# Graph attention with layer norm on one core: the last group of edges in two parts, and blocks of nodes finished four turns behind instead of five

## The reference

```python
Q, K, V = (x @ WQ, x @ WK, x @ WV)           # 8 heads of 16
E = edge_attr @ WE
score = exp(clip(sum_d(K[src] * Q[dst] * E) / 4, -5, 5))       # one per edge and head
h = segment_sum(V[src] * score, dst) / (segment_sum(score, dst) + 1e-6)
out = layernorm(x + h)
```

## Time and profile before

| | before |
|---|---|
| median of three executions | 2052.68 us |
| profiled execution, its own time | 2051.81 us |
| its span | 2050.0 us |
| POOL busy | 1531.1 us (75%), 1629 instructions |
| PE busy | 1521.4 us (74%) |
| DVE busy | 1488.4 us (73%) |
| ACT busy | 1386.6 us (68%) |
| DMA, mean rate | 174 GB/s |
| mean granted clock of PE | 0.892 of full |

### The profile page before, as it was taken

How to read it: one execution, slowest core, us unless ns; L and a number is a source line. 1 busy time by engine, 2 the same in 40 slices (tenths; PEclk the granted TensorE clock), 3 DMA queues, 4 the chain that set the end, 5 groups by cost and what they waited for, 6 DMA issues and landing times.

```text
span 2050.0 us, 40006 instructions
## 1 busy us (share of the span) xinstructions
PE 1521.4 (74%) x10440; PEld 1267.1 (62%) x10441; DVE 1488.4 (73%) x3809; ACT 1386.6 (68%) x3716; POOL 1531.1 (75%) x1629
## 2 busy tenths in 40 slices
PE   7788887778787776776677767677776777778674
PEld 6566666666666665665565556566665656666564
DVE  5577777878787776777677767767776776777676
ACT  4478786768777766666666666666666666666663
POOL 7777777777777777777777777777777777777774
PEclk9889898999899989889989989988889989888887
DMA  9668666666666665566566556656655655555552
GB/s 296 202 193 240 171 180 169 178 172 181 170 180 177 172 167 166 166 171 168 166 167 170 168 163 169 173 166 167 166 169 162 173 167 172 162 171 166 166 167 83
DMA packets 281410, 356.31 MB, mean 174 GB/s; under 512 B 144640, under 2 KB 177615, under 8 KB 281186
## 3 DMA queue, kind: packets, MB, share of 16 engines
q0 software_dynamic: 76864, 209.29, 35.3%
q1 hardware_dynamic: 203746, 144.18, 25.7%
q10 hardware_dynamic: 576, 0.26, 0.0%
HBM read 337.59 MB, written 15.97 MB: 172 GB/s over the span
## 4 chain that ended last, share of the span: by engine, by line
PE 24%; issue 21%; DVE 19%; POOL 17%; DMA 10%; DVEq 8%; ACT 0%; SPq 0%; POOLq 0%; ACTq 0%
POOL kv L560 17%; PE psW L712 13%; DMA kv<-kv_table,src_idx 9%; DVEq L286 6%; DVE msg L1105 6%; DVE acc L1121 5%; PE psE L691 4%; DVE prod L1089 3%; PE psT L675 3%; DVEq L1121 2%; PE psF L683 1%; PE psE L635 1%; DVE score L1094 1%; DVE newton L1159 1%; DMA q_table<-q_stage 1%
## 5 line engine op out<-in xcount | busy, mean ns | idle before, releaser
L560 POOL DMA_INDIRECT kv<-kv_table,src_idx x1580 | 1495.2, 946 | 485.6 <-issue 416.1
L712 PE MATMUL psW<-msg,hot 128*128 128x136 f32 x3224 | 539.0, 317 | 485.0 <-DVE msg L1105 483.9
L712 PEld LDWEIGHTS psW<-msg,hot 128*128 128x128 f32 x3224 | 462.3, 214 | 534.1 <-issue 509.2
L1084 DVE TENSOR_TENSOR prod<-kv,psE 128x512 f32<-128x512 f32 x403 | 275.5, 684 | 368.4 <-issue 186.3
L851 ACT ACTIVATE hot<-iota,local 128x128 f32<-128x128 f32 x1612 | 508.7, 386 | 0.0
L691 PE MATMUL psE<-w_e,attrT 128*128 128x128 f32 x3224 | 502.3, 302 | 0.0
L691 PEld LDWEIGHTS psE<-w_e,attrT 128*128 128x128 f32 x3224 | 423.6, 205 | 106.5 <-issue 106.5
L873 ACT ACTIVATE psW<-clipped 128x32 f32<-128x32 f32 x403 | 81.0, 201 | 571.4 <-DVE clipped L1100 564.3
L1121 DVE TENSOR_TENSOR acc<-psW,acc 64x136 f32 x806 | 238.0, 295 | 110.1 <-PE psW L712 102.2
L856 ACT ACTIVATE hot<-hot,one 128x512 f32<-128x512 f32 x403 | 291.0, 722 | 13.1
L1089 DVE TENSOR_TENSOR prod<-prod,psQ 128x512 f32<-128x512 f32 x403 | 277.1, 688 | 12.8 <-PE psQ L701 0.2
(11 more groups left out here) (118 smaller groups left out, 546.0 us busy)
## 6 DMA issues: line engine op xcount, KB each, us to landing
attr<-in_edge_attr_dram SPq DMA_DIRECT2D x403, 256.0 KB
kv<-kv_table,src_idx POOLq DMA_INDIRECT x1580
q_near<-q_table SPq DMA_DIRECT2D x403, 32.0 KB
kv_table<-kv SPq DMA_DIRECT2D x12, 512.0 KB, 4.9
q_table<-q_stage SPq DMA_DIRECT2D x12, 384.0 KB, 3.2
hot<-in_x_dram SPq DMA_DIRECT2D x12, 256.0 KB, 5.2
xT<-in_x_dram SPq DMA_DIRECT2D x8, 384.0 KB
out_dram<-xT SPq DMA_DIRECT2D x45, 64.0 KB
```

Source lines behind the costliest of these rows:

```text
L560: nc.gpsimd.indirect_dma_start(out=kv[:, g % RINGS, t, :], out_offset=None, in_=kv_table, in_offset=bass.IndirectOffsetOnAxis(ap=src_idx[: ...
L712: last = nc.tensor.matmul(psW[:, g % 2, 0:MW], hot[:, g % HOTS, t, :], msg[:, g % MSGS, t, :], start=(t == 0), stop=(t == TILES - 1))
L1084: nc.vector.tensor_tensor(tiles, kv[:, u, :, 0:dim], psE[:, g % 2, :].rearrange("p (t d) -> p t d", d=dim), ALU.mult).then_inc(ke, 1)
```

## The change

- The last group (402) is worked in two parts, tiles 0 to 2 and tile 3, on DVE, ACT and PE. `last_scores` and `last_messages` are `scores` and `messages` on the tiles of one part. The gather of tile 3 has a semaphore of its own, kv_last; its exponentials go to psT, as psW's bank is in use. The tail of DVE's program is ordered anew by two `meanwhile` functions.
- LAG becomes 4: 46 blocks are finished in the loop, block w in turn w + 4, and LATE becomes 3. The table's base is written 2(1 - LAG), the same number as before; the cap 2 EARLY becomes 92. DVE waits for `added` ahead of a block's first stage, and for the block's third stage ahead of the next group's addition.
- DVE loads the number of strays together with the last half windows, SP loads redo_cell ahead of its wait for the last blocks.

```diff
-LAG = 5
+LAG = 4
...
+        def last_exp_scores(part):
+            if part == 0:
+                return exp_scores(G - 1)[:, 0:TILES - 1, :]
+            return psT[:, 0:HEADS].rearrange("p (t h) -> p t h", h=HEADS)
...
@@ SP's program @@
+            redo = sp.value_load(redo_cell, min_val=0, max_val=G)
             sp.wait_ge(finished, (EARLY + 1) * STAGES)
...
-            with sp.If(sp.value_load(redo_cell, min_val=0, max_val=G) > 0):
+            with sp.If(redo > 0):
...
@@ POOL's program @@
-                           [[2, B_LAST], [0, TURN]], base=2 * (2 - LAG), channel_multiplier=0)
+                           [[2, B_LAST], [0, TURN]], base=2 * (1 - LAG), channel_multiplier=0)
...
+                    landed = kv_last if g == G - 1 and t == TILES - 1 else kv_in[g % RINGS]
...
@@ PE's program @@
+            def sum_last():
+                pe.wait_ge(hot_ok, G)
+                pe.wait_ge(added, G - 2)
+                for t in range(TILES):
+                    if t == 0:
+                        pe.wait_ge(heads_ok, G)
+                        pe.wait_ge(msg_ok, G)
+                    elif t == TILES - 1:
+                        pe.wait_ge(heads_ok, G + 1)
+                        pe.wait_ge(msg_ok, G + 1)
+                    last = nc.tensor.matmul(psW[:, (G - 1) % 2, 0:MW], hot[:, (G - 1) % HOTS, t, :],
+                                            msg[:, (G - 1) % MSGS, t, :], start=(t == 0), stop=(t == TILES - 1))
+                last.then_inc(sums, 1)
...
-            sum_messages(G - 1)
+            sum_last()
...
@@ ACT's program @@
+            def exponentials_last(part):
+                tiles = slice(0, TILES - 1) if part == 0 else slice(TILES - 1, TILES)
+                act.wait_ge(clip, G + part)
...
+                nc.scalar.activation(last_exp_scores(part), scores, ACT.Exp, scale=SCALE).then_inc(exp_ok, 1)
+                if part == 0:
+                    act.wait_ge(sums, G - MSGS)
+                nc.scalar.activation(msg[:, (G - 1) % MSGS, tiles, dim:MW], scores, ACT.Exp, scale=SCALE)\
+                    .then_inc(heads_ok, 1)
...
@@ DVE's program @@
+            def last_scores(part, meanwhile):
+                g = G - 1
+                u, tiles = g % RINGS, slice(0, TILES - 1) if part == 0 else slice(TILES - 1, TILES)
...
+                if part == 0:
+                    dve.wait_ge(e_mm, G)
+                    dve.wait_ge(kv_in[u], KV_WITHOUT_LAST)
+                else:
+                    dve.wait_ge(kv_last, 16)
...
             def step(g, windows, w=None):
                 def meanwhile(i):
+                    if w is not None and (u, i) == (1, 0):
+                        dve.wait_ge(finished, w * STAGES + 3)
                     if i == 0 and g >= 2:
                         add_sums(g - 2, windows)
                     if i == 1 and g >= 1:
                         messages(g - 1)
+                    if w is not None and 3 * u + i == 0:
+                        dve.wait_ge(added, g - 1)
                     if w is not None and 3 * u + i < STAGES:
                         finish(3 * u + i, w, 1, window_y[:, :, :], finished, w * STAGES)
...
             windows = load_windows(B_LAST * TURN - 2, G - B_LAST * TURN + 2)
-            for g in range(B_LAST * TURN, G):
+            strays = dve.value_load(table[0:1, STRAYS, G:G + 1], min_val=0, max_val=G)
+            for g in range(B_LAST * TURN, G - 1):
                 step(g, windows[g - B_LAST * TURN])
-            messages(G - 1)
-            add_sums(G - 2, windows[-2])
+            def meanwhile_first(i):
+                if i == 0:
+                    add_sums(G - 3, windows[-3])
+                elif i == 1:
+                    messages(G - 2)
+            def meanwhile_second(i):
+                if i == 0:
+                    last_messages(0)
+                elif i == 1:
+                    add_sums(G - 2, windows[-2])
+            last_scores(0, meanwhile_first)
+            last_scores(1, meanwhile_second)
+            last_messages(1)
             add_sums(G - 1, windows[-1])
...
-            dve.wait_ge(table_ok, 1)
-            with dve.If(dve.value_load(table[0:1, STRAYS, G:G + 1], min_val=0, max_val=G) > 0):
+            with dve.If(strays > 0):
```

More of the change, by code:

```diff
@@ L241, in graph_attention_layernorm @@
         kv_in = [sem(f"kv_in{i}") for i in range(RINGS)]
+        kv_last = sem("kv_last")
         go = sem("go")
@@ L292, in exp_scores @@
             return psW[:, g % 2, GROUP // 2:GROUP // 2 + TILES * HEADS].rearrange("p (t h) -> p t h", h=HEADS)
+        def last_exp_scores(part):
+            if part == 0:
+                return exp_scores(G - 1)[:, 0:TILES - 1, :]
+            return psT[:, 0:HEADS].rearrange("p (t h) -> p t h", h=HEADS)
+        KV_WITHOUT_LAST = ((G - 1) // RINGS + 1) * TILES * 16 - 16
         def per_head(ap):
@@ L559, in gather @@
                         continue
+                    landed = kv_last if g == G - 1 and t == TILES - 1 else kv_in[g % RINGS]
                     nc.gpsimd.indirect_dma_start(
                         out=kv[:, g % RINGS, t, :], out_offset=None, in_=kv_table,
-                        in_offset=bass.IndirectOffsetOnAxis(ap=src_idx[:, g, t:t + 1], axis=0))\
-                        .then_inc(kv_in[g % RINGS], 16)
+                        in_offset=bass.IndirectOffsetOnAxis(ap=src_idx[:, g, t:t + 1], axis=0)).then_inc(landed, 16)
             for g in range(G):
@@ L876, in exponentials @@
                 nc.scalar.activation(msg[:, g % MSGS, :, dim:MW], scores, ACT.Exp, scale=SCALE).then_inc(heads_ok, 1)
+            def exponentials_last(part):
+                tiles = slice(0, TILES - 1) if part == 0 else slice(TILES - 1, TILES)
+                act.wait_ge(clip, G + part)
+                scores = clipped[:, :].rearrange("p (t h) -> p t h", h=HEADS)[:, tiles, :]
+                nc.scalar.activation(last_exp_scores(part), scores, ACT.Exp, scale=SCALE).then_inc(exp_ok, 1)
[3 more added lines that the diff above has]
+                    .then_inc(heads_ok, 1)
             def step(g):
@@ L895, in _ @@
                 mark(g)
-            for g in range(G):
+            for g in range(G - 1):
                 step(g)
+            for part in range(2):
+                exponentials_last(part)
             act.wait_ge(table_ok, 1)
@@ L1107, in messages @@
                                         ALU.mult).then_inc(msg_ok, 1)
+            def last_scores(part, meanwhile):
+                g = G - 1
+                u, tiles = g % RINGS, slice(0, TILES - 1) if part == 0 else slice(TILES - 1, TILES)
+                columns = slice(tiles.start * dim, tiles.stop * dim)
+                heads = slice(tiles.start * HEADS, tiles.stop * HEADS)
+                if part == 0:
[3 more added lines that the diff above has]
+                    dve.wait_ge(kv_last, 16)
+                products = prod[:, columns].rearrange("p (t d) -> p t d", d=dim)
+                nc.vector.tensor_tensor(products, kv[:, u, tiles, 0:dim],
+                                        psE[:, g % 2, columns].rearrange("p (t d) -> p t d", d=dim), ALU.mult)\
+                    .then_inc(ke, 1)
+                meanwhile(0)
+                dve.wait_ge(ke, G + part)
+                dve.wait_ge(q_sel, G)
+                nc.vector.tensor_tensor(prod[:, columns], prod[:, columns], psQ[:, g % 2, columns], ALU.mult)\
+                    .then_inc(keq, 1)
+                meanwhile(1)
+                dve.wait_ge(keq, G + part)
+                if part == 0:
+                    dve.wait_ge(clip, g)
+                nc.vector.tensor_reduce(score[:, heads], prod[:, columns].rearrange("p (a d) -> p a d", d=DH), AX.X,
+                                        ALU.add).then_inc(dot, 1)
+                dve.wait_ge(dot, G + part)
+                if part == 0:
+                    dve.wait_ge(heads_ok, g)
+                nc.vector.tensor_scalar(clipped[:, heads], score[:, heads], SCORE_LIMIT / SCALE, -SCORE_LIMIT / SCALE,
+                                        ALU.min, ALU.max).then_inc(clip, 1)
@@ new lines, in last_messages @@
+            def last_messages(part):
+                g = G - 1
+                tiles = slice(0, TILES - 1) if part == 0 else slice(TILES - 1, TILES)
+                dve.wait_ge(exp_ok, G + part)
+                nc.vector.tensor_tensor(per_head(msg[:, g % MSGS, tiles, 0:dim]),
+                                        per_head(kv[:, g % RINGS, tiles, dim:2 * dim]),
+                                        last_exp_scores(part).unsqueeze(3)
+                                        .to_broadcast([P, tiles.stop - tiles.start, HEADS, DH]),
+                                        ALU.mult).then_inc(msg_ok, 1)
```

## The result

The changed kernel takes 2050.03 us, the median of 22 executions (2047.28 to 2055.92), and the kernel before, run between them, 2052.63 (22 executions, 2051.25 to 2055.72). The ratio is 0.9987, with a 95% interval from 0.9981 to 0.9993: 2.6 us less, 0.13%. The forecast was 2.4 us less. The spread of single executions doubled (standard deviation 2.15 us for 1.10). Most kernels of experiments 5 to 7 first ran in a set where every kernel, the one before too, took 2594 to 2683 us; those runs are left out.

What follows compares the result with a forecast made beforehand. POOL's queue of gathers was taken to set 96% of the span, with a 20.3 us tail behind it; 0.3 + 0.6 + 0.83 + 0.65 + 0.1 - 0.1 = 2.4 us gave 2050.3 us by the median, range 2048.6 to 2052.9.

Steps and rivals of the forecast that it cites:

- within 0.2%: The chance that the time lies within 0.2% (4.1 us) of no change, put at 0.88; faster 0.09, slower 0.03.
- a: Last group in two parts: DVE starts three tiles 1.25 us sooner; gain 0.3 us, between -0.3 and 1.0.
- f: One more block finished in turn five: computation 1.4 us later from group 40, holding POOL at group 125; loss 0.1, ends 0 and 2.0.
- b: DVE's load of the strays moved from behind the last addition to the last half windows: gain 0.6 us, between 0.5 and 0.7.
- d: SP's load of the redo flag moved ahead of its wait for the last block: gain 0.65 us, between 0.6 and 0.75.
- c: Three windows instead of four finished behind the strays, all on the path: gain 0.83 us, between 0.6 and 1.0.
- e: Store of whole late windows carries two instead of three, 128 KB for 192: gain 0.1 us, between 0 and 0.3.
- the prediction's own signs of being wrong: A tail from the last gather's start outside 20.3 to 21.2 us, or POOL's stretch of gathers longer by over 1 us.
- rival (3): Slower: a larger hold of POOL at group 125, losing from a lag of 3.9 us on; up to 2053.6 us; chance 0.05.
- rival (1): The added block's lag reaches POOL: the whole 1.4 us or more comes through, time 2051.6 us; chance 0.22.
- The rule on the shared port: GpSimd cannot write descriptors during DVE's two-port modes, so a block's final scaling holds POOL some 0.3 us; sum 2.1 instead of 2.4.
- Rival (2): PE's clock stays high at the end, so splitting the last group gains 1.0 us: 2049.6 us, or 2048.6; chance 0.12.

Runs made afterwards that it cites:

- experiment 5: The changed kernel with SETTLED = 146 for 125 (more distance for POOL) and LAG = 5 for 4: 2050.81 us, the kernel before 2053.15.
- experiment 6: The changed kernel with SETTLED = 146 and the loads of the last half windows and of the strays at the start of turn 49: 2049.50 us, ratio 0.9981.
- experiment 7: The changed kernel with SETTLED = 146 and the last group whole again: first with the loads at turn 51, 2052.92 us; second at turn 49, 2053.34; before 2055.58.
- experiment 1: The changed kernel with LAG = 5 again, so without the added block: 2050.15 us, the kernel before 2052.76.
- experiment 2: The kernel before with LAG = 4 alone, its two waits and its table: 2052.76 us, ratio 0.9998.
- experiment 3: The changed kernel with SETTLED = 146 for 125, letting POOL run three groups further ahead of PE at groups 97 to 125: 2049.73 us, ratio 0.9986.
- experiment 4: The kernel before with SETTLED = 146 for 125, the same added distance for POOL: 2053.16 us, ratio 1.0001.

## Why the prediction was right, point by point

The forecast was 2050.3 us and the measurement is 2050.03; this, its sign, its range and its "within 0.2%" held. That it came so close is in part luck: a was put too small and f too small, and the two errors cancelled. The medians say it too. Without LAG = 4 (experiment 1, with a, b and d) the gain was 2.6 us where the terms give 1.55; LAG = 4 alone (experiment 2, with c, e and f) gained 0.0 where they give 0.83; both together gained 2.6. Each of the two experiments is uncertain by 1.8 us. And both of the prediction's own signs of being wrong were met in the profiled execution, the longest of 22: a tail of 21.4 us and gathers longer by 6.2. In experiment 3 they were not (21.1 us, and gathers 0.4 us shorter).

The ends of its sum were added wrongly. The upper ends of a to e make 3.75 us, which is 2048.9 and not 2048.6; the lower ends, with f's 2.0 and b's 0.25, make a loss of 0.85, which is 2053.5 and not 2051.5. So the range that ends at 2052.9 was narrower than the prediction's own terms.

**a, the parts: 0.3 us, between -0.3 and 1.0.** Experiment 7 gives 0.4 with the loads at turn 51 and 1.4 with them at turn 49, neither clear of its interval. The working took the landing of the last gather from one row (1.60 us of idling, 2.79 behind the start). That row is nearly the best case: of some 140 groups from 160 on at which DVE waited for its gather in that trace, the wait ended 2.76 to 5.38 us behind the start of the group's last gather, median 3.05. At the end of the span the rows came 3.7 to 4.3 us behind it in four of ten profiles. The parts hide this, and the prediction did not count it. Their 1.25 us at the start is real only if DVE is there: in the changed kernel and in experiments 1, 3 and 5 it came 2.5, 3.8, 1.9 and 2.2 us behind the last gather's start.

**b, the load of the strays: 0.6.** 0.63 in each profile that has the move. "So nothing, at most 0.25" for its new place was too sure. The cover that it named, DVE's idle time ahead of groups 401 and 402, was a trait of the profiled execution: in the changed kernel and in experiments 1, 3 and 5 it was 0.1 us at most, and in experiment 4, whose tail is that of the kernel before, 0.05. In experiment 7's first kernel there were 3.0 us of it again. The idle time ahead of group 400, where the load now stands, grew from 2.51 to 3.14 us. What that costs in time was not settled.

**c, three late blocks: 0.83.** 7.09 to 6.25 us, 0.84; 6.27 in experiment 2. Right in the profiles; the medians can't show it.

**d and e, SP's load and the store: 0.65 + 0.1.** From the last stage's end to the span's end it was 4.77 us before, 4.13 and 4.05 with d alone (experiments 1 and 5), 4.41 with e alone (experiment 2) and 3.56 to 3.66 with both. So d is 0.65 to 0.8 and e 0.35 to 0.55. The term e was mis-sized: from the last stage's end to the span's end it is more than the "0.1, between 0 and 0.3".

**f, the added block: -0.1, between 0 and -2.0.** The mechanism (a later computation reaches POOL where its distance falls) and its place were right, and so was the block's own lag: the fifth turn took 35.4, 35.3 and 35.4 us for 34.1 without the block (prediction: 1.4 later). The size was off. "With 0.1 to 0.2 for a start" should have been 0.75, which takes half of the slack of 1.54 away. The tightest point was not group 125 either: at group 20 the gather started 0.84 behind its projection. The prediction looked for the smallest slack only where the distance shrinks. With 1.3 of lag and 0.79 of free slack the hold would be 0.5 in an execution like the profiled one.

The 4.37 us have another source besides. Counted from the first gather, the projection that group 125 follows ended 5.2 us later than before (640.81 less 51.23, against 635.96 less 51.62), and only 1.3 of them are the added block's turn. Most of the rest is three turns, the 11th, 13th and 15th, of 36.7 to 36.8 us where the kernel before had 34.7, 35.8 and 35.2. In each of them two of PE's sums in a row ran at half clock behind DVE's register loads, and in the shorter turns one did. The pair of the 11th turn:

```profile
455.94 2.15 PE L721 MATMUL psW<-msg,hot 128*128 128x136 f32 x8 [4.34 <-DVE msg L1140]
...
461.70 2.13 PE L721 MATMUL psW<-msg,hot 128*128 128x136 f32 x8
```

By these numbers (5.2 less 1.3 less 0.79) some 3.1 us of hold would have come without the block, an estimate. Among turns 6 to 16 there were 4, 0, 3, 2, 3 and 1 such pairs in the six profiles with LAG = 4 and 1, 1, 0 and 0 in the four with LAG = 5; whether the added block or the two extra waits bring them about stays open. The slack itself differs by 4 us between executions (1.54 before, 3.65 in experiment 2, 5.59 in experiment 1, at the same group and distance), and the four profiles at the old distance have holds of 0, 4.37, 0 and 0.32 us (before, changed, experiments 1 and 2). So the changed kernel's one long execution that was seen is the case of rival (3), holds of 4.37 us against a gain of some 2.5; the median is neither that nor rival (1).

**The rule on the shared port** (the Trainium skill, "SBUF — State Buffer", section "Who interferes with whom") would have the added block's scaling hold POOL. In the changed kernel the seven longer gaps all lie where the distance to PE binds, and experiment 3, with the added block but with more distance, has none: the trace still does not agree.

**Rival (2)**, the clock at the end, was asked of one sum and concerns the whole tail: the sums of groups 397 to 401 took 1.15 us or up to 2.15 (2.4 or 1.2 GHz) in changing mixtures. In nine of ten profiles those of group 401 were slow, as the prediction took them (1.75 to 2.15; 1.17 in experiment 5). The tail is between 9.98 and 12.50 us in ten profiles. The profile before has the shortest of them, so the prediction read its rows from a favourable tail: in experiments 4 and 2, whose kernels are the same from the last gather to the last addition, it was 10.7 and 11.3.

**The sum.** With a 0.4 by the medians and by the profiles b 0.63, c 0.84, d 0.67 and e 0.45, it is 3.0 us, against 2.6 measured, and 3.0 under the kernel before in experiment 3, where nothing holds POOL. That would leave about 0.4 for f at the median, a remainder well inside the intervals. The prediction had 2.5 and 0.1.

What stays open: how often executions are held and by how much, what LAG = 4 brings by itself (0.0 by experiment 2, 0.7 to 1.2 by experiments 3 and 5, all within their intervals), what the strays' load costs at its new place, and whether experiment 6's kernel beats the changed one (0.9981 [0.9972, 0.9990] against 0.9987 [0.9981, 0.9993]).

## What to carry to other kernels

Where one queue paces a kernel by itself, cut the span at its last instruction: what is moved out of the tail can be read from the profile to 0.05 us (b and c here), though medians with intervals of 1 to 2 us neither show nor refute it. What it is moved to must be held against the smallest slack that the pacing queue has anywhere, and that slack must be counted from the delay with which the queue starts behind an event that it has waited for (0.75 us here), not from zero. One profiled execution gives one draw of that slack and of the tail, so look at how the same wait varies over all its repetitions in the trace before taking a single row as its length. Register loads are small work, but right ahead of the end they stopped DVE for 2.3 to 3.1 us, and in three of the eight profiles that have them there PE's sums of group 399 ran at half clock; in the two without they did not.

## What the runs showed of the hardware that was not expected

- A gather on POOL started 0.75 us after the end of the projection it waited for, six times within 0.03 us in the changed kernel, where DVE's additions start about 0.2 us behind PE's sums and PE 0.25 behind DVE.
- A group's rows landed 2.76 to 5.4 us behind the start of its last gather. At the end of the span, where little else moves, they landed by 3.2 us except in the four profiles with an instruction packet of 16 KB beside them (3.7 to 4.3).
- Two executions of the same loop differ by 4 us in how far computation is behind POOL at group 125, though single instructions on DVE, ACT and POOL take the same time to 0.02 us. From the 6th turn on, the sums right behind DVE's register loads took 1.6 to 2.15 us instead of 1.17 in 448 of 450 turns of the ten profiles; the turns of 36.8 us instead of 34.9 have a second sum at half clock behind it.
